# The Gram product from rounded rows with one cross term, and the attention's weights turned by VectorE from squares

## What is computed

```
x = x + 0.5 * ffn(layernorm(x))
x = x + attn(layernorm(x))
x = x + 0.5 * ffn(layernorm(x))
```

```
a   = einsum('bthd,bshd->bhts', q, k)
ctx = einsum('bhts,bshd->bthd', a, v)
g   = ctx.transpose(0, 2, 3, 1)
mean, var = g.mean(axis=(2, 3)), ((g - mean) ** 2).mean(axis=(2, 3))
ctx = (g - mean) * rsqrt(var + EPS) * gn_w + gn_b ;  out = ctx @ out_w.T + out_b
```

## Time and profile before

| | |
|---|---|
| median of 3 runs | 640.37 us (639.58 to 640.39) |
| profiled execution, its own time | 640.34 us |
| its span | 638.6 us |
| TensorE busy | 632.5 us, 99% of the span |
| VectorE busy | 520.0 us, 81% |
| GpSimd busy | 463.9 us, 73% |
| ScalarE busy | 394.4 us, 62% |
| TensorE's granted clock | 1.00 |

### The profile page before, as it was taken

How to read it: one execution, slowest core, us unless ns; L and a number is a source line. 1 busy time by engine, 2 the same in 40 slices (tenths; PEclk the granted TensorE clock), 3 DMA queues, 4 the chain that set the end, 5 groups by cost and what they waited for, 6 DMA issues and landing times.

```text
span 638.6 us, 9958 instructions
## 1 busy us (share of the span) xinstructions
PE 632.5 (99%) x2905; PEld 524.7 (82%) x2905; DVE 520.0 (81%) x1572; ACT 394.4 (62%) x784; POOL 463.9 (73%) x401
## 2 busy tenths in 40 slices
PE   8999999999999999999999999999999999999997
PEld 7787888888888888888888888888888888888886
DVE  6898878787977879778797797977988878787674
ACT  4866656556575665756667556675565656565553
POOL 6997876777677677776767767686677777767664
PEclk9999999999999999999999999999999999999999
DMA  8726372543638335383353733637436362450710
GB/s 234 263 84 246 86 265 51 166 136 78 236 86 230 115 98 202 83 230 119 89 210 83 223 123 73 246 84 196 159 76 252 66 246 71 150 181 21 279 33 34
DMA packets 128343, 94.26 MB, mean 148 GB/s; under 512 B 84113, under 2 KB 110625, under 8 KB 128289
## 3 DMA queue, kind: packets, MB, share of 16 engines
q1 hardware_dynamic: 128288, 93.63, 47.1%
HBM read 81.55 MB, written 12.06 MB: 147 GB/s over the span
## 4 chain that ended last, share of the span: by engine, by line
PE 93%; POOL 5%; ACT 1%; issue 0%; DVE 0%; DVEq 0%; POOLq 0%
PE gateP L559 10%; PE gateP L563 10%; PE gateP L560 10%; PE yP L563 10%; PE yP L560 10%; PE yP L559 10%; PE upP L559 10%; PE upP L560 10%; PE upP L563 10%; POOL A_lo L431 3%; POOL W_lo L424 2%; PE attP L644 1%; PE yP L693 1%; PE backP L678 1%; PE attP L678 1%; PE backP L629 1%
## 5 line engine op out<-in xcount | busy, mean ns | idle before, releaser
L431 POOL TENSOR_TENSOR A_lo<-A,A_hi 128x512 fp32r<-128x512 f32 x287 | 369.7, 1297 | 121.3 <-ACT A_hi L933 120.8
L959 ACT ACTIVATE gateP<-gateP 128x512 f32<-128x512 f32 x252 | 146.5, 581 | 187.2 <-PE gateP L563 186.6
L1398 DVE TENSOR_TENSOR T<-gateP,CB 128x512 f32<-128x512 f32 x252 | 173.5, 689 | 88.7 <-ACT gateP L959 86.1
L933 ACT CAST A_hi<-A 128x512 fp32r<-128x512 f32 x287 | 175.9, 613 | 11.9 <-DVE A L1459 11.1
L1459 DVE TENSOR_TENSOR A<-upP,T 128x512 f32<-128x512 f32 x254 | 173.4, 683 | 3.0
L559 PE MATMUL gateP<-XT_hi,W_hi 128*128 128x512 f32 x288 | 115.5, 401 | 0.0
L559 PE MATMUL yP<-A_hi,W_hi 128*128 128x512 f32 x288 | 112.5, 391 | 0.0
L563 PE MATMUL gateP<-XT_lo,W_hi 128*128 128x512 f32 x288 | 112.3, 390 | 0.0
L563 PE MATMUL yP<-A_lo,W_hi 128*128 128x512 f32 x288 | 112.2, 390 | 0.0
L560 PE MATMUL gateP<-XT_hi,W_lo 128*128 128x512 f32 x288 | 112.2, 390 | 0.0
L560 PE MATMUL yP<-A_hi,W_lo 128*128 128x512 f32 x288 | 112.1, 389 | 0.0
(11 more groups left out here) (244 smaller groups left out, 623.3 us busy)
## 6 DMA issues: line engine op xcount, KB each, us to landing
CB<-combT SPq DMA_DIRECT2D x126, 512.0 KB, 7.1
y_rows<-YB SPq DMA_DIRECT2D x60, 64.0 KB, 1.9
YP<-y_rows SPq DMA_DIRECT2D x15, 256.0 KB, 2.7
x_rows<-XN SPq DMA_DIRECT2D x13, 256.0 KB, 2.3
XB<-x_rows SPq DMA_DIRECT2D x52, 64.0 KB, 2.3
xa_rows<-XA SPq DMA_DIRECT2D x4, 512.0 KB, 4.1
W_in<-xa_rows SPq DMA_DIRECT2D x16, 128.0 KB, 2.9
out_dram<-X SPq DMA_DIRECT2D x7, 256.0 KB, 8.3
```

What stands on the lines that cost most here:

```text
L431: pool.tensor_tensor(A_lo[:, slot, :], A[:, slot, :], A_hi[:, slot, :].bitcast(F32), ALU.subtract).then_inc(low_done, 1)
L933: act.copy(A_hi[:, v % SLOTS, :], A[:, v % SLOTS, :]).then_inc(high_done, 1)
L959: act.activation(dst, gateP[u % 2][:, :], ACT.Silu).then_inc(silu_done, 1)
L1398: dve.tensor_tensor(T[:, u % TS, :], silu, weights, ALU.mult).then_inc(gate_weighted, 1)
```

## The change

1. **Rounded rows.** XA's rows are rounded to XH's first half (ScalarE, units 8 and 9) and the rest goes to its second half (GpSimd, units 9 and 11). One matmul of 256 columns a tile gives H^T H and H^T L side by side; L^T L is left away. The Gram matrix is H^T H + H^T L + (H^T L)^T. The transposed term is never formed: Gn, which is only used in a quadratic form, takes H^T L twice, and the product Wk G Wv^T gets its third part from HL as stationary operand: HL by WkT (unit 14), copied to Q (ScalarE, unit 16), by WvT (unit 17).
2. **The sums.** VectorE adds up the tiles of each half to XS (units 8 and 10), and TensorE adds the partitions with two matmuls by a column of ones.
3. **Places.** The product moves from unit 11 to 12, the copy from 12 to 13, GS and Gn are made by VectorE, ScalarE's normalisation of XN is split between units 10 and 11. XA, XS, GS, Q, s_row and HL now lie in parts of W_in, which is free by then.
4. **The weights** of the attention come as squares (eight transfers in place of three) and VectorE turns them, at unit 32 of the first pair. TensorE's transposes and ScalarE's copies of them are gone. The transposes of XN for step 2 now stand ahead of down(13), directly behind those of the combined weights.

```diff
@@ sync
+            for lo, hi, matrix in ((0, 2 * P, Wqkv_w[P:3 * P]), (2 * P, 3 * P, out_w)):
+                squares = matrix.rearrange("(m c) (b r) -> b c m r", c=SQUARE, r=SQUARE)
+                for i in range(P // SQUARE):
+                    sp.dma_start(turned_in[i * SQUARE:(i + 1) * SQUARE, lo:hi].rearrange("c (m r) -> c m r", r=SQUARE),
+                                 squares[i]).then_inc(small_in, 16)
@@ gpsimd
+                    if attention and u in (9, 11):
+                        h = (u - 9) // 2
+                        pool.wait_ge(xa_high, 2 * (p - ATT0) + h + 1)
+                        half_tiles = slice(h * TILES, (h + 1) * TILES)
+                        pool.tensor_tensor(XH[:, half_tiles, 1, :], XA[:, half_tiles, :],
+                                           XH[:, half_tiles, 0, :].bitcast(F32), ALU.subtract).then_inc(xa_low, 1)
@@ tensor
-                if u == 11:
-                    pe.wait_ge(xa_ready, b + 1)
+                if u == 12:
+                    pe.wait_ge(xa_summed, 2 * (b + 1))
+                    for h in range(2):
+                        pe.matmul(attP[:, 2 * P:2 * P + 1], XS[:, h, :], ones[:, 0:1], start=(h == 0), stop=(h == 1))
+                    pe.wait_ge(xa_low, 2 * (b + 1))
                     for j in range(BT):
-                        mm = pe.matmul(attP[:, 0:P + 1], XA[:, j, 0:P], XA[:, j, :],
+                        mm = pe.matmul(attP[:, 0:2 * P], XH[:, j, 0, :], XH[:, j, :, :].rearrange("p h d -> p (h d)"),
                                        start=(j == 0), stop=(j == BT - 1))
                 if u == 14:
+                    pe.matmul(attP[:, 3 * P:4 * P], HL[:, 0:P], WkT[:, :], start=True, stop=True)
                 if u == 17:
-                    pe.matmul(attP[:, 0:P], WkT[:, :], P1[:, :], start=True, stop=True).then_inc(att_pe, 1)
+                    pe.wait_ge(att_act, ATT_ACT * b + 3)
+                    pe.matmul(attP[:, 0:P], WkT[:, :], P1[:, :], start=True, stop=False)
+                    pe.matmul(attP[:, 0:P], Q[:, :], WvT[:, :], start=False, stop=True).then_inc(att_pe, 1)
                     if first and u == UNITS - 1:
                         transpose_weights(1)
+                        transpose_next(2)
-                    if first and u == 20:
-                        for i, matrix in enumerate((Wk_in, Wv_in, Wo_in)):
-                            mm = pe.transpose(attP[:, i * P:(i + 1) * P], matrix[:, :], ident[:, :])
-                    if early and w == 17:
-                        transpose_next(2)
@@ scalar
+                if u == 9:
+                    act.wait_ge(xa_half, 2 * (b + 1))
+                    act.copy(XH[:, TILES:BT, 0, :], XA[:, TILES:BT, :]).then_inc(xa_high, 1)
+                if u == 8:
+                    act.wait_ge(xa_half, 2 * b + 1)
+                    act.copy(XH[:, 0:TILES, 0, :], XA[:, 0:TILES, :]).then_inc(xa_high, 1)
-                    if w in ((15, 16) if early else (10 if attention and s == 0 else 9,)) and not last:
-                        for part in (w - 15,) if early else (0, 1):
+                    if w in ((15, 16) if early else (10, 11) if attention and s == 0 else (9,)) and not last:
+                        for part in (w - 15,) if early else (w - 10,) if attention and s == 0 else (0, 1):
@@ vector
+                if u in (8, 10):
+                    h = (u - 8) // 2
+                    dve.wait_ge(xa_half, 2 * b + h + 1)
+                    dve.tensor_reduce(XS[:, h, :], XA[:, h * TILES:(h + 1) * TILES, :].rearrange("p j d -> p d j"),
+                                      AX.X, ALU.add).then_inc(xa_summed, 1)
                 if u == 13:
+                    dve.tensor_tensor(GS[:, :], attP[:, 0:P], HL[:, 0:P], ALU.add).then_inc(gram_seq, 1)
+                    dve.scalar_tensor_tensor(Gn[:, :], HL[:, 0:P], 2.0, attP[:, 0:P], ALU.mult,
+                                             ALU.add).then_inc(gram_seq, 1)
+                    if first and u == PAIR - 4:
+                        dve.wait_ge(small_in, 16 * 15)
+                        dve.transpose(turned[:, :], turned_in[:, :]).then_inc(weights_turned, 1)
```

More of the change, by code:

```diff
@@ L150, in macaron_kernel @@
         Wq = sb("Wq", [P, P + 1])
[L151 to L156, removed]
+        turned_in = sb("turned_in", [P, 3 * P])
+        turned = sb("turned", [P, 3 * P])
+        WkT, WvT, WoT = (turned[:, i * P:(i + 1) * P] for i in range(3))
         bk = sb("bk", [P, 1])
@@ L195, in macaron_kernel @@
         XAB = W_in[:, 0:3, :, :].rearrange("p u i d -> p (u i d)")[:, 0:BT * P]
+        XA = W_in[:, 6:9, :, :].rearrange("p u i d -> p (u i) d")[:, 0:BT, :]
+        spare = W_in[:, 9:12, :, :].rearrange("p u i d -> p (u i d)")
+        XS = spare[:, 0:2 * P].rearrange("p (h d) -> p h d", h=2)
+        GS, Q, s_row, HL = (spare[:, 2 * P:3 * P], spare[:, 3 * P:4 * P], spare[:, 4 * P:5 * P],
+                            spare[:, 5 * P:6 * P + 1])
         XAT = W_in[:, 3:6, :, :].rearrange("p u i d -> p (u i) d")[:, 0:BT, :]
@@ L245, in macaron_kernel @@
         att_act = sem("att_act")
-        xa_ready = sem("xa_ready")
+        xa_half, xa_high, xa_low = sem("xa_half"), sem("xa_high"), sem("xa_low")
+        xa_summed, gram_seq = sem("xa_summed"), sem("gram_seq")
         xa_stored, xa_in, xat_ready = sem("xa_stored"), sem("xa_in"), sem("xat_ready")
@@ L504, in pair @@
                                            RT4[:, :, :, 0].bitcast(F32), ALU.subtract).then_inc(router_split, 1)
-                    if first and u == 24:
-                        pool.memset(XA[:, :, :], 1.0)
                     if w == (14 if early else 3) and not last:
@@ L647, in attention_stage @@
                 if u == 14:
-                    pe.wait_ge(att_act, ATT_ACT * b + 3)
-                    pe.matmul(attP[:, 0:P], GS[:, 0:P], WvT[:, :], start=True, stop=True)
+                    pe.wait_ge(att_act, ATT_ACT * b + 2)
+                    pe.wait_ge(gram_seq, 2 * (b + 1))
+                    pe.wait_ge(weights_turned, 1)
+                    pe.matmul(attP[:, 0:P], GS[:, :], WvT[:, :], start=True, stop=True)
                     pe.matmul(attP[:, P:2 * P], s_row[:, :], WvT[:, :], start=True, stop=True)
+                    pe.matmul(attP[:, 3 * P:4 * P], HL[:, 0:P], WkT[:, :], start=True, stop=True)
                     pe.matmul(attP[:, 2 * P:3 * P], s_row[:, :], ident[:, :],
@@ L891, in attention_stage @@
                                              scale=arstd[:, j:j + 1], bias=ashift[:, j:j + 1])
-                    if u == 9:
-                        ins.then_inc(xa_ready, 1)
-                if u == 12:
+                        if j % TILES == TILES - 1:
+                            ins.then_inc(xa_half, 1)
+                if u == 9:
[4 more added lines that the diff above has]
+                    act.copy(XH[:, 0:TILES, 0, :], XA[:, 0:TILES, :]).then_inc(xa_high, 1)
+                if u == 13:
                     act.wait_ge(att_pe, ATT_PE * b + 1)
-                    act.copy(GS[:, :], attP[:, 0:P + 1]).then_inc(att_act, 1)
-                if u == 13:
+                    act.copy(HL[:, :], attP[:, P:2 * P + 1]).then_inc(att_act, 1)
                     act.wait_ge(att_act, ATT_ACT * b + 1)
                     act.activation(s_row[:, :], ones[:, :], ACT.Identity,
-                                   scale=GS[:, P:P + 1]).then_inc(att_act, 1)
-                    act.activation(Gn[:, :], attP[:, 0:P], ACT.Identity,
-                                   scale=1.0 / SEQ).then_inc(att_act, 1)
+                                   scale=HL[:, P:P + 1]).then_inc(att_act, 1)
+                if u == 16:
+                    act.wait_ge(att_seq, ATT_OPS * b + 10)
+                    act.copy(Q[:, :], attP[:, 3 * P:4 * P]).then_inc(att_act, 1)
                 if u == 20:
@@ L971, in pair @@
                                  ).then_inc(router_split, 1)
[L972 to L977, removed]
                     if first and u in (3, 4):
```

25 lines of the change are left out of this document (10 added, 15 removed).

## The result

| | before | changed |
|---|---|---|
| median | 639.93 us (5 runs) | 643.94 us (5 runs) |
| profiled execution | 640.34 us, span 638.6 | 644.17 us, span 642.4 |

The ratio is 1.0059, with a 95% interval of 1.0046 to 1.0071: slower by 3.8 us. The forecast was 644.2. One of the changed kernel's five runs took 1400.04 us at the same granted clock, for a reason that stays open: it counts in the median above and not in the ratio, and the other four have a median of 643.73 (643.42 to 644.17).

A forecast was written before the change was run, and what follows sets the result against it. TensorE, busy for 99% of the span, was taken to bound the kernel. 640.34 us profiled + 0.35 setup + 4 batches x (0.05 own work + 0.82 waits) = 644.2 us, range 640.6 to 647.

The forecast's parts named there:

- The cover: Units 11 and 12: moved Gram product no longer hides ScalarE's delay, so A(10) is late for up(12); 0.82 us a batch.
- the queue's delay: ScalarE, units 8 and 9: two roundings and a wait for the last XA make silu(10) 1.1 us later.
- four for A and four for T: Profile sign: TensorE waits four times some 0.5 us for VectorE's A and four times some 0.3 for T.
- TensorE's own work: Per batch: cheaper Gram product against column sums and two small products, -1.79 + 0.95 + 0.45 + 0.44 = +0.05 us.
- The first pair: Setup: weight transposes save 0.33 us, XN's transposes ahead of down(13) cost 0.68; together +0.35 us.
- The wait for XN: Setup: TensorE waits for ScalarE's XN with down(13) no longer filling the time; 0.68 us, all on the path.
- The reductions: VectorE, units 8 and 10: two reductions of 128x512 taken at 0.69 us each, hidden.
- the room of 0.85: VectorE, unit 8: its queue has 0.85 us free for the reduction until silu(9) lets it go on.
- The cover holds: Rival: silu(10) comes less than 0.29 us late, so no wait at up(12); 640.9 us, chance 0.15.
- narrow matmuls are nearly free: Rival: the one-column sums cost almost nothing instead of 0.45 us; 642.4 or 642.8 us, chance 0.08, plus 0.05 with no stall.
- The reductions are slow: Rival: VectorE's reductions read elements 512 bytes apart and take up to 2.1 us, delaying the array; 649.8 us, chance 0.12.
- the 1.2 us up to which the prediction had silu(10) decide: VectorE: at a reduction of 1.2 us T(9) moves 0.35 us, still behind silu(10)'s delay.

The follow-up runs named there:

- e4: The kernel before with two copies of 128x512 added on ScalarE per batch, Gram product left at unit 11: 640.02 us, 1.0004.
- e5: The kernel before with both the two added ScalarE copies and the Gram product moved to unit 12: 642.69 us, 1.0045.
- e6: The kernel before with only its Gram product moved from unit 11 to 12 and ScalarE's copy of it to 13: 639.69 us, 0.9998.
- e1: The changed kernel without ScalarE's two roundings of XA in each batch (XH's high half filled once, group variance set to 1): 640.98 us, 1.0016.
- e2: The changed kernel without VectorE's two reductions in each batch (XS filled once with ones): 643.88 us, 1.0060.
- v1: The changed kernel with XN's transposes back behind down(13), second rounding at unit 10, Gram product split over units 11 and 12: 640.29 us, 1.0006.
- e7: The changed kernel without both ScalarE's two roundings and VectorE's two reductions in each batch: 640.19 us, 1.0006.
- after_again: The changed kernel, unaltered, run once more beside the others on one chip: 643.75 us, 1.0061.
- e3: The changed kernel with the transposes of XN for step 2 back behind down(13) in the first pair: 643.45 us, 1.0053.
- v2: The kernel before with the weights' part alone: squares loaded, turned by VectorE, TensorE's three transposes gone, XN's transposes unmoved: 639.47 us, 0.9994.
- e8: The changed kernel with VectorE's two reductions adding four neighbouring elements instead of four lying 512 bytes apart: 643.73 us, 1.0060.

## Why the prediction was right

**The cover (0.82 us a batch).** Right in place, cause and size. The array loses 0.52 us at up(12) and by the same reading 0.22 at gate(12), where the forecast had 0.52 and 0.3; some 0.14 at unit 11, which it did not have, make it 0.88. That it takes both the queue's delay and the moved product is shown by e4, e5 and e6. ScalarE's roundings as the cause are shown by e1 against e2. Less exact were the waits foretold, four for A and four for T: the list has 12 and 11, smaller ones among them.

**TensorE's own work (+0.05 us a batch).** Right, in sum and in its terms: the new group takes the 1.40 us of the forecast. The rounded matmuls start at 190.27, 0.36 us behind the first one-column record, but that start isn't the price of the one-column pair: the first matmul behind a full-precision group is stretched, and the second rounded one starts at 190.47, 0.20 on, where the others follow at 0.12. By the rule of the prediction, from the second matmul behind, the pair costs 190.47 - 189.91 - 0.12 = 0.44 us, and v1 gives 0.45; the eight rounded ones are left with 0.96. The floor of the Trainium skill (TensorE: Matmul & The Clock Gate, Back-to-back issue gap) that I had set beside them, some 25 ns for so few columns, isn't what this kernel pays: 0.11 us a record was measured, each with its own load of weights. The two small products take 0.22 and 0.23. e7, which has all of this work and no wait at units 11 and 12, takes 241.07 us for the three batches below, 0.01 a batch more than before.

**Both together.** A stretch of three batches, from a gate at 239.97 to the same one at 481.02, takes 241.05 us before and 243.88 after (241.04 to 484.92): 0.94 a batch, where I had 0.87. That the total was met within 0.03 us in the profiled execution is luck in part: these stretches and the first pair give 4 x 0.94 + 0.37 = 4.1 us, not the 3.8 of the forecast, and the profile taken after had reached gate(17) 0.24 us sooner than the one before (46.45 against 46.69), a place that differs from profile to profile (46.15 in after_again).

**The first pair (+0.35).** The wait for XN is there, and it costs 0.69 (e3) where I had 0.68; the weights' transposes give 0.33 back, by the forecast and by v2's profile. From gate(17) to gate(32) the changed kernel takes 0.37 longer than before (32.55 and 32.92 us).

**The reductions.** The term that was mis-sized: I took 0.69 us, the product's time, and it was 1.09. That is over the room of 0.85, so T(9) came late and unit 11 lost its 0.14 us, which I had at nothing; without the reductions (e2) and with faster ones (e8) it loses nothing. It didn't matter for the time, because silu(10) was later still. Had ScalarE's roundings been cheap, this would have been the error: e1 against e7 puts it at 0.8 us, 0.2 a batch. In e1 I had allowed for more, 0.2 to 0.4 a batch with what else was left, and expected 641.5 to 642.2 where 641.0 was measured.

**The rivals.** "The cover holds" and "narrow matmuls are nearly free" fell by the rows above. "The reductions are slow" was right in its mechanism (e8), and the size was too small to change the time: at 1.09 us they stayed under the 1.2 us up to which the prediction had silu(10) decide.

## What to carry to other kernels

Where one engine is busy for 99% of the span, ask of each group of work on it what waits it covers: the old product's 1.8 us were at the same time the slack of ScalarE and VectorE, and the added work and the moved place, each free by itself, took it away together. Test such a pair by doing each alone and then both; a sum that is larger than its parts names the cover. And a cheaper product that needs small extra ones has to be counted with them: 0.83 us saved on the Gram product (1.79 to 0.96) became a loss of 0.05 with 0.44 for the sums and 0.44 for two small products, and a gain only in the version in which the sums cost nothing.

## What the runs showed of the hardware

A reduction of 128x512 to 128x128 on VectorE takes 1.09 us when the four elements that are added lie 512 bytes apart and 0.68 when they are neighbours (e8). The Trainium skill (SBUF — State Buffer, Door 1: The DMA port swizzle) states a penalty for accesses that cross to a new line of 16 bytes; the runs agree that such a reading is slower, by 0.41 us for 512 elements. They compare these two orders alone, so that the line of 16 bytes is the reason isn't shown.

A full-precision matmul costs 0.11 us a record, two records each, at 1 column (v1) as at 16 and 129; a narrow output saves nothing.

The type of the matmuls beside a group matters a little: with full-precision matmuls in it, the first record behind the group is stretched (0.47 to 0.48 us in place of 0.39); a group of rounded matmuls leaves no trace of that (0.39 to 0.40).
